# Self edges of a three-layer relational GNN: from gathered rows to a mask on VectorE over the rows just made

## The chip, the cores and the metric

One core of one Trainium2 chip (trn2). The metric is the device time of one execution in microseconds, median of three runs. Engines: PE (TensorE), DVE (VectorE), ACT (ScalarE), POOL (GpSimd), SP (the sync engine, which issues DMAs).

## What is computed

N = 3125 nodes, D = 128 features, E = 103,125 edges sorted by destination, R = 16 relation types, H = 4 attention heads, three layers. The edge list is 50,000 random pairs in both directions and then one edge from each node to itself; the sort is stable, so in every node's list the self edge is the last one.

```python
for l in range(L):
    ht = jnp.einsum('nd,rdo->nro', h, W_rel[l])
    msg = ht[src, etype]
    h_rel = jax.ops.segment_sum(msg, dst, num_segments=n)
    h_rel = h_rel + h @ W_loop[l] + b_rel[l]
    z = (h @ W_gat[l]).reshape(n, H, DH)
    el = jnp.sum(z * attn_l[l], axis=-1)
    er = jnp.sum(z * attn_r[l], axis=-1)
    e = jax.nn.leaky_relu(el[src] + er[dst], 0.2)
    # softmax of e over the edges of each dst (with its maximum), alpha
    h_gat = jax.ops.segment_sum(alpha[:, :, None] * z[src], dst, num_segments=n)
    hc = jnp.concatenate([h_rel, h_gat + b_gat[l]], axis=1) @ W_fuse + b_fuse
    # layer 0 only: hc = hc * sigmoid([hc, mean edge weight] @ W_gate + b_gate)
    h = jax.nn.relu(hc)
```

The output is layernorm(x + h).

## The kernel before

A table in HBM holds, for each node and type, a row of 260 floats: the 128 of the message ht, then for each head 32 of z and its el. An edge is one gathered row. Two tables alternate: layer l reads `table[l % 2]`, and the next layer's is written while layer l runs.

Until about 214 us the kernel loads, counts degrees, ranks the nodes by degree (descending), writes the first table tile by tile (PE, ACT, SP), gathers each node's list of edges, masks the lists (L1262 to L1267) and scatters lists and node data to `meta_ranked` in order of rank (L561). From there on it runs three layers of 25 tiles of 128 ranked nodes (tile 0 has 64 nodes, each on two partitions, and its halves are merged). I count layers one, two and three (l = 0, 1, 2) and tiles from 0. A tile has as many slots as its largest degree (tile 0: half of it). For the drawn graph that is 29, 45, 42, 40, 39, 38, 37, 36, 36, 35, 35, 34, 33, 33, 32, 32, 31, 30, 30, 29, 28, 27, 26, 25, 23: 825 in all.

**POOL** (L683 to L715) issues one indirect DMA for each slot (`fetch`, L593 to L596): row k of the list of 128 nodes into slot k of a buffer. A tile is split into groups: H with 16 slots in the buffer `meta_nat`, where there are 32 slots or more M1 with 16 in `late`, and the rest (1 to 15) as T in `scratch`, the tail. The names in the profile are those of the buffers. Before a group it waits until VectorE has staged its list of indices (`stage_head`, `stage_mid`, `stage_tail`) and until the last group in that buffer is summed (`free`). Behind H, from tile 2 on, it issues the store of the next layer's rows of two tiles earlier (`store_tile`, L671), in layers one and two.

**VectorE** in each tile (L1475 to L1513): clears the tail's slots and stages the tail's list (`stage_this_tail`, L1337), copies er (`start_tile`), runs `group` for H, then `epilogue` of the tile before (in layer one the gate, in layer three the layernorm), then `group` for M1 and T. A group waits for its gathers, computes logits and their maximum, carries the sums so far in slot 0, sums the messages (L1371), multiplies z by the weights that ACT put in PSUM (L1377) and sums that (L1381). T is computed for 15 slots, or for 8 where it has 8 or fewer. `end_tile` (L1396 to L1401) hands the sums to PE, with the loop term of `meta` added.

**ACT** gives each group its exponentials (`group`, L786), and in each tile the chain of the tile before: transposed sums, fused, gate, and `next_rows` (L810), which empties PE's table of the next layer into `rows[0]` and lets POOL store it. Through a layer's end this chain is passed once with nothing beside it: the next layer gathers only when all rows are stored (L723).

The wait that sets the tail's place on POOL is this:

```python
pool.wait_ge(s_tail, n_tile)     # L701, stage_tail written by VectorE
...
with pool.If(bits(pool, n, PAIR - 1) > 0):
    free("T")
    gather_tail(l, n, PAIR // 2)
```

## Time and profile before

| | |
|---|---|
| median of 3 runs | 3485.82 us (3484.82 to 3485.93) |
| the profiled execution: span, first to last instruction | 3490.2 us |
| its own device time | not listed apart; the span stands for it |
| POOL busy | 2489.3 us, 71% |
| VectorE busy | 2380.3 us, 68% |
| PE, ACT busy | 689.4 us, 424.8 us |
| gathers (indirect DMAs of L594) | 2475: 1200 + 720 + 555 |
| layers one, two, three | 214 to 1316 us, 1316 to 2412 us, 2412 us to the end |

POOL's busy time counts the making of each DMA's descriptors only, and the idle time between two DMAs issued back to back is told as "issue". The profiled execution is 4.4 us, 0.13%, above the median.

### The profile page before, as it was taken

How to read it: one execution, taken by the hardware profiler on the slowest of the kernel's cores; microseconds unless marked ns; L12 is line 12 of the kernel's file. 1: busy time of each engine (PE TensorE's matmuls, PEld its weight loads, DVE VectorE, ACT ScalarE, POOL GpSimd, SP SyncE). 2: the span in 40 equal slices, each digit the busy share in tenths (PEclk: the TensorE clock that was granted, in tenths of full speed). 3: DMA queues.
4: the chain of work that ended last, by engine and by line, in shares of the span. 5: the costliest groups of instructions: out<-in, count | busy, mean ns of one | idle time of the engine just before them, and what ended most of it. 6: DMA issues, size and time to landing. Idle time of an engine off the chain costs nothing.

```text
span 3490.2 us, 18122 instructions
## 1 busy us (share of the span) xinstructions
PE 689.4 (20%) x1897; PEld 372.5 (11%) x1897; DVE 2380.3 (68%) x3226; ACT 424.8 (12%) x769; POOL 2489.3 (71%) x2642
## 2 busy tenths in 40 slices
PE   8942111222122230011121111221000000000000
PEld 5421000111011110000000000110000000000000
DVE  8536666677676764665777756674776788877786
ACT  3530110111111120101111111111000000000000
POOL 1457777777777756777777777775777777777776
PEclk9965555555655555555555555555555555555555
DMA  7774444455545544444454544454433333333332
GB/s 271 315 249 129 134 147 152 152 151 152 152 152 159 168 145 118 130 151 152 151 152 151 153 152 152 152 173 140 107 106 107 107 106 107 106 106 107 106 103 74
DMA packets 143244, 505.96 MB, mean 145 GB/s; under 512 B 44277, under 2 KB 51002, under 8 KB 133618
## 3 DMA queue, kind: packets, MB, share of 16 engines
q0 software_dynamic: 130032, 444.45, 43.4%
q1 hardware_dynamic: 13186, 61.24, 4.5%
q14 instruction: 19, 0.16, 0.0%
q8 instruction: 7, 0.11, 0.0%
HBM read 341.05 MB, written 164.51 MB: 145 GB/s over the span
## 4 chain that ended last, share of the span: by engine, by line
POOL 45%; issue 29%; DVE 10%; DMA 6%; PE 4%; POOLq 3%; DVEq 1%; ACT 1%; SPq 1%; ACTq 0%
POOL meta_nat L594 20%; POOL late L594 14%; POOL scratch L594 10%; DVE acc L1381 3%; PE ps_table L886 1%; DMA late<-table,stage_mid 1%; DMA table<-rows 1%; DMA scratch<-table,stage_tail 1%; DVE late L1377 1%; DVE scratch L1377 1%; DVE meta_nat L1377 1%; POOLq L369 1%; POOL table L671 1%; DMA meta_nat<-table,stage_head 1%; PE ps_cnt L919 1%
## 5 line engine op out<-in xcount | busy, mean ns | idle before, releaser
L594 POOL DMA_INDIRECT meta_nat<-table,stage_head x1200 | 1139.0, 949 | 395.7 <-issue 385.3
L594 POOL DMA_INDIRECT late<-table,stage_mid x720 | 681.9, 947 | 219.4 <-issue 217.9
L594 POOL DMA_INDIRECT scratch<-table,stage_tail x555 | 525.9, 948 | 175.5 <-issue 175.2
L1025 PE MATMUL ps_mix<-ident,hr 128*128 128x128 f32 x75 | 35.5, 473 | 1991.2 <-DVE hg L1401 1991.2
L788 ACT ACTIVATE ps_cnt<-logit 128x68 f32<-128x68 f32 x189 | 43.7, 231 | 2767.1 <-DVE logit L1363 2766.1
L1381 DVE TENSOR_REDUCE acc<-meta_nat 128x132 f32<-128x2112 f32 x75 | 290.6, 3875 | 8.1 <-DVE meta_nat L1377 0.5
L1371 DVE TENSOR_REDUCE acc<-meta_nat 128x128 f32<-128x2048 f32 x75 | 282.6, 3767 | 0.0
L1049 PE MATMUL ps_table<-wrel,hT 128*128 128x512 f32 x400 | 266.4, 828 | 0.0
L1353 DVE TENSOR_TENSOR raw<-late,er_cur 128x64 f32<-128x64 f32 x45 | 12.0, 267 | 324.5 <-DMA late<-table,stage_mid 324.5
L1025 PEld LDWEIGHTS ps_mix<-ident,hr 128*128 128x128 f32 x75 | 13.6, 182 | 2039.8 <-DVE hg L1401 2039.8
L1381 DVE TENSOR_REDUCE acc<-scratch 128x132 f32<-128x1188 f32 (+1 forms) x69 | 208.7, 3024 | 7.1
L1353 DVE TENSOR_TENSOR raw<-meta_nat,er_cur 128x64 f32<-128x64 f32 x75 | 20.1, 267 | 281.6 <-DMA meta_nat<-table,stage_head 280.2
L1371 DVE TENSOR_REDUCE acc<-scratch 128x128 f32<-128x1152 f32 (+1 forms) x69 | 204.9, 2970 | 8.8
L1381 DVE TENSOR_REDUCE acc<-late 128x132 f32<-128x2244 f32 x45 | 183.3, 4072 | 4.7
L1371 DVE TENSOR_REDUCE acc<-late 128x128 f32<-128x2176 f32 x45 | 178.2, 3961 | 5.5
L1334 DVE MEMSET scratch<- 128x1024 f32 (+1 forms) x75 | 93.0, 1240 | 125.5 <-issue 125.5
L1377 DVE TENSOR_TENSOR meta_nat<-meta_nat,ps_cnt 128x2112 f32<-128x2112 f32 x75 | 175.8, 2344 | 3.1 <-ACT ps_cnt L788 3.1
L742 ACT ACTIVATE rows<-ps_table 128x1024 f32<-128x1024 f32 x150 | 148.8, 1026 | 100.2 <-PE ps_table L886 62.4
L1049 PEld LDWEIGHTS ps_table<-wrel,hT 128*128 128x128 f32 x400 | 115.3, 288 | 136.6 <-issue 126.3
L1377 DVE TENSOR_TENSOR scratch<-scratch,ps_cnt 128x1188 f32<-128x1188 f32 (+1 forms) x69 | 127.2, 1843 | 0.0
L1377 DVE TENSOR_TENSOR late<-late,ps_cnt 128x2244 f32<-128x2244 f32 x45 | 111.7, 2482 | 0.0
L1031 PE MATMUL ps_mix<-hrT,wfuse 128*128 128x128 f32 x100 | 39.8, 501 | 363.6 <-ACT hgT L794 363.6
(237 smaller groups left out, 1701.4 us busy)
## 6 DMA issues: line engine op xcount, KB each, us to landing
table<-rows SPq DMA_DIRECT2D x25, 2080.0 KB, 7.7
meta_nat<-table,stage_head POOLq DMA_INDIRECT x1200, 2.8
late<-table,stage_mid POOLq DMA_INDIRECT x720
scratch<-table,stage_tail POOLq DMA_INDIRECT x555, 2.8
meta<-meta_ranked SPq DMA_DIRECT2D x1, 2438.0 KB, 15.1
wrel<-in_L_gnn_W_rel POOLq DMA_DIRECT2D x2, 1024.0 KB, 13.5
meta_nat<-in_x SPq DMA_DIRECT2D x1, 832.0 KB, 18.4
table<-rows,stage_id POOLq DMA_INDIRECT x50, 7.8
```

Source lines behind the costliest of these rows:

```text
L369: n = eng.value_load(tile_slots[0:1, bass.ds(t, 1)], min_val=PAIR, max_val=E)
L594: pool.indirect_dma_start(out=slots[b][:, k, :], out_offset=None, in_=table[l % 2], in_offset=bass.IndirectOffsetOnAxis(ap=index, axis=0)) ...
L671: pool.indirect_dma_start(out=table[(l + 1) % 2][0:NP_ * R, :].rearrange("(n r) f -> n (r f)", r=R), out_offset=bass.IndirectOffsetOnAxis( ...
L742: return s.activation(rows[k][:, j * R // 2:(j + 1) * R // 2, 0:D], ps_table[:, 1024 * j:1024 * j + 1024].rearrange("p (r f) -> p r f", f= ...
L788: s.activation(wgt[:, :, :, 0], logit[:], ACT.Exp).then_inc(s_wgt, 1)
L1025: pe.transpose(mix[0], hr[:], ident[:])
L1031: pe.matmul(mix[2], wfuse[:, 0], hrT[:], start=True, stop=False)
L1049: mm = pe.matmul(ps_table[:, 512 * c:512 * c + 512], hT[0][:], wrel[:, l + 1, c * RC * D:(c + 1) * RC * D], start=True, stop=True)
L1334: v.memset(messages("T", 1, slots_of_tail + 1), 0.0)
L1371: v.tensor_reduce(acc[:, 0:D], messages(b, lo, K + 1).rearrange("p k d -> p d k"), AX.X, ALU.add).then_inc(s_part, 1)
L1377: v.tensor_tensor(weighted(b, lo, K + 1), weighted(b, lo, K + 1), wgt[:, lo:K + 1].to_broadcast([P, K + 1 - lo, H, EX]), ALU.mult).then_in ...
L1381: v.tensor_reduce(acc[:, D:ROW], slots[b][:, lo:K + 1, D:ROW].rearrange("p k f -> p f k"), AX.X, ALU.add).then_inc(s_acc, 1)
```

## The change

Four things, word for word below. First, before the layers VectorE finds in each list of rank 128 and above the last entry, tests that it is the node's own, takes it out of the list and out of the degree, and puts it in a new column `M_OWN`. Second, layer one gathers that column as a group of one into slot 0 of H (`gather_head`), so H has 17 slots there. Third, layers two and three do not gather it: ACT keeps z of each tile's nodes in `own_z` (which takes the place of `rows[1]`), VectorE copies it into slot 0 at the tile's start, and at the end of each tile but the first, ahead of `end_tile`, `add_own_messages` multiplies the finished `rows[0]` of the tile before by a one-hot of each node's own type, sums over the 16 types and adds the result to the loop term of the next layer. Fourth, ACT runs `next_rows` ahead of the third group's exponential instead of behind it, and waits there until VectorE's mask has read the rows. For tile 0's nodes (ranks below 128) nothing is taken out. `yo` moves into the room of `wrel`.

```diff
+            def gather_head(l):
+
+                if l == 0:
+                    pool.indirect_dma_start(
+                        out=slots["H"][:, 0, :], out_offset=None, in_=table[l % 2],
+                        in_offset=bass.IndirectOffsetOnAxis(ap=stage_head[:, 0:1], axis=0)).then_inc(s_own_landed, 16)
+                gather(l, "H", stage_head[:, 1:PAIR + 1])
...
                 free("H")
-                gather(l, "H", stage_head)
+                gather_head(l)
                 if l < L - 1:
                     with pool.If(t > 1):
                         store_tile(l)
...
                     act.reg_add(n_stored, n_stored, 16)
+                    act.wait_ge(s_own_rows, n_own)
+                    act.reg_add(n_own, n_own, 1)
                     act.wait_ge(s_z_ps, n_tab)
                     s.activation(rows[0][:, :, D:ROW], bc(ps_z[:, 0:D + H], R), ACT.Copy)
                     for j in range(2):
                         evacuate_half(0, j)
+                    s.activation(own_z[:, bass.ds(t, 1), :], ps_z[:, 0:D + H].rearrange("p (o f) -> p o f", o=1), ACT.Copy)
                     s.activation(meta[:, bass.ds(t, 1), M_ER:META],
                                  ps_z[:, D + H:ZW].rearrange("p (o f) -> p o f", o=1), ACT.Copy).then_inc(s_rows, 1)
                     act.reg_add(n_tab, n_tab, 1)
 
...
                 with act.If(groups > 1):
                     group()
-                    with act.If(groups > 2):
-                        group()
                 if not first:
                     next_rows(l, act.snap(n_last, min_val=0, max_val=T - 1))
                     act.reg_add(n_last, n_last, 1)
+                with act.If(groups > 2):
+                    group()
...
+            step(v.tensor_scalar(may_drop, rank[:], float(P), None, ALU.is_ge))
             for i, (t0, t1) in enumerate(ELL_CHUNKS):
+                lists, codes = meta_nat[:, t0:t1, M_ELL:SCATTERED], last_codes[:, 0:t1 - t0]
+                code, gap, own, gone = (a[:, t0:t1] for a in (last_code, apart, is_own, dropped))
                 dve.wait_ge(s_ell[i], 16 * (t1 - t0))
-                step(v.scalar_tensor_tensor(meta_nat[:, t0:t1, M_ELL:SCATTERED], ell_int[:, t0:t1], -float(NULL),
-                                            ell_valid[:, t0:t1], ALU.add, ALU.mult))
-                v.tensor_scalar(meta_nat[:, t0:t1, M_ELL:SCATTERED], meta_nat[:, t0:t1, M_ELL:SCATTERED], float(NULL), None,
...
-                                ALU.add).then_inc(s_ell_ok, 1)
...
+                step(v.scalar_tensor_tensor(lists, ell_int[:, t0:t1], -float(NULL), ell_valid[:, t0:t1], ALU.add, ALU.mult))
+                step(v.tensor_tensor(codes, lists, is_last[:, t0:t1], ALU.mult))
+                step(v.tensor_reduce(code, codes, AX.X, ALU.add))
+                step(v.tensor_tensor(gap, code, own_at[:, t0:t1], ALU.subtract))
+                step(v.tensor_tensor(gone, gap, gap, ALU.mult))
+                step(v.scalar_tensor_tensor(own, gone, 0.25 * R * R, may_drop[:, t0:t1], ALU.is_lt, ALU.mult))
+                step(v.tensor_tensor(gone, code, own, ALU.mult))
+                v.tensor_tensor(codes, is_last[:, t0:t1], bc_last(gone, ELL), ALU.mult)
+                step(v.tensor_tensor(degree[:, t0:t1], degree[:, t0:t1], own, ALU.subtract))
+                v.tensor_scalar(meta_nat[:, t0:t1, M_OWN], gone, float(NULL), None, ALU.add)
+                v.tensor_copy(meta_nat[:, t0:t1, M_CNT], degree[:, t0:t1])
+                v.scalar_tensor_tensor(lists, lists, float(NULL), codes, ALU.add, ALU.subtract).then_inc(s_ell_ok, 1)
...
-            def group(b, first=False, meanwhile=None, K=PAIR):
-
-                lo = 1 if first else 0
+            def group(b, first=False, meanwhile=None, K=PAIR, own_gathered=False):
+
+                lo = 1 if first and not own_gathered else 0
+                new = 0 if first else 1
                 dve.wait_ge(s_landed[b], n_land[b])
                 if b != "T":
                     dve.reg_add(n_land[b], n_land[b], 16 * K)
+                if own_gathered:
+                    dve.wait_ge(s_own_landed, n_own_land)
+                    dve.reg_add(n_own_land, n_own_land, 16)
...
                 dve.wait_ge(s_product, n_g)
-                v.tensor_reduce(acc[:, D:ROW], slots[b][:, lo:K + 1, D:ROW].rearrange("p k f -> p f k"), AX.X, ALU.add
...
             def start_tile(l, t):
                 if l == 0:
                     dve.wait_ge(s_er, n_t)
+                else:
+                    z = own_z[:, bass.ds(t, 1), :].rearrange("p o (h e) -> p (o h) e", e=EX)
+                    v.tensor_copy(weighted("H", 0, 1)[:, 0, :, 0:DH], z[:, :, 0:DH])
+                    v.tensor_scalar(weighted("H", 0, 1)[:, 0, :, DH], z[:, :, DH], no_own[:, bass.ds(t, 1)], None, ALU.add)
                 v.tensor_copy(er_cur[:], meta[:, bass.ds(t, 1), M_ER:M_LOOP]).then_inc(s_tile, 1)
                 dve.wait_ge(s_tile, n_t)
...
+            def add_own_messages(l, t):
+
+                if l < L - 1:
+                    dve.wait_ge(s_rows, n_rows)
+                    dve.reg_add(n_rows, n_rows, 1)
+                    v.tensor_tensor(own_rows[:], rows[0][:, :, 0:D],
+                                    own_hot[:, bass.ds(t, 1), :].rearrange("p o (r f) -> p (o r) f", f=1
+                                                                           ).to_broadcast([P, R, D]), ALU.mult
+                                    ).then_inc(s_own_rows, 1)
+                    dve.wait_ge(s_own, n_own)
+                    dve.wait_ge(s_own_rows, n_masked)
+                    dve.reg_add(n_masked, n_masked, 1)
+                    v.tensor_reduce(own_sum[:], own_rows[:].rearrange("p r d -> p d r"), AX.X, ALU.add
+                                    ).then_inc(s_own_sum, 1)
+                    dve.wait_ge(s_own_sum, n_own)
+                    dve.reg_add(n_own, n_own, 1)
+                    loop = meta[:, bass.ds(t, 1), M_LOOP:META].rearrange("p o f -> p (o f)")
+                    v.tensor_tensor(loop, loop, own_sum[:], ALU.add).then_inc(s_own, 1)
...
-                group("H", first=True, meanwhile=lambda: stage_next_head(t))
+                group("H", first=True, meanwhile=lambda: stage_next_head(t), own_gathered=l == 0)
                 if not first:
                     epilogue(l, dve.snap(n_last, min_val=0, max_val=T - 1))
-                    dve.reg_add(n_last, n_last, 1)
...
                     merge_halves(l)
+                else:
+                    add_own_messages(l, dve.snap(n_last, min_val=0, max_val=T - 1))
+                    dve.reg_add(n_last, n_last, 1)
                 end_tile(t)
...
                 epilogue(l, T - 1)
+                add_own_messages(l, T - 1)
```

Names with `own_` that are not shown are buffers and semaphores. With the last entry taken out of each list, tiles 1 to 24 have one slot less each (44, 41, 39, 38, 37, 36, 35, 35, 34, 34, 33, 32, 32, 31, 31, 30, 29, 29, 28, 27, 26, 25, 24, 22), 801 with tile 0.

VectorE, the end of a tile in the loop over tiles of layer one; before:

```order
L1377 TENSOR_TENSOR scratch<-scratch,ps_cnt 128x9x132 [waits weights_ready,peak_kept]
L1381 TENSOR_REDUCE acc<-scratch 128x132 [waits weighted_z_ready,messages_summed]
L1383 REGISTER_ALU
L1509 UNCONDITIONAL_BRANCH
L1396 RECIPROCAL rden<-acc 128x4 [waits sums_updated]
L1397 ISA
L1397 TENSOR_TENSOR hr<-acc,meta 128x128
L1400 REGISTER_ALU [waits denominators_inverted]
L1401 TENSOR_TENSOR hg<-acc,rden 128x128
```

and now:

```order
L1435 TENSOR_TENSOR scratch<-scratch,ps_cnt 128x9x132 [waits weights_ready,peak_kept]
L1439 TENSOR_REDUCE acc<-scratch 128x132 [waits weighted_z_ready,messages_summed]
L1441 REGISTER_ALU
L1594 UNCONDITIONAL_BRANCH
L1475 ISA [waits rows_ready]
L1476 TENSOR_TENSOR own_rows<-rows,own_hot 128x2048
L1482 REGISTER_ALU [waits own_messages_masked,own_messages_added_to_loop_term]
L1483 TENSOR_REDUCE own_sum<-own_rows 128x128
L1486 ISA [waits own_messages_summed]
L1488 TENSOR_TENSOR meta<-meta,own_sum 128x128
L1600 REGISTER_ALU
L1458 RECIPROCAL rden<-acc 128x4 [waits sums_updated]
```

Three instructions on 2048, 2048 and 128 elements and a wait for ACT's rows stand between the last group and `end_tile`; the rows of tail staging for the next tile come behind them all.

ACT, from the second group's exponential to the end of `next_rows` in the same loop; before:

```order
L788 ACTIVATE ps_cnt<-logit 128x68 [waits logits_ready]
L789 REGISTER_ALU
L838 COMPARE_AND_BRANCH
L788 ACTIVATE ps_cnt<-logit 128x68 [waits logits_ready]
L789 REGISTER_ALU
L838 UNCONDITIONAL_BRANCH
L814 REGISTER_ALU [waits rows_stored]
L816 ACTIVATE rows<-ps_z 128x16x132 [waits z_product_ready]
L742 ACTIVATE rows<-ps_table 128x8x128 [waits table_chunk1_ready]
L742 ACTIVATE rows<-ps_table 128x8x128 [waits table_chunk3_ready]
L819 ISA
L819 ACTIVATE meta<-ps_z 128x132
```

and now:

```order
L816 ACTIVATE ps_cnt<-logit 128x68 [waits logits_ready]
L817 REGISTER_ALU
L868 UNCONDITIONAL_BRANCH
L842 REGISTER_ALU [waits rows_stored]
L844 REGISTER_ALU [waits own_messages_masked]
L846 ACTIVATE rows<-ps_z 128x16x132 [waits z_product_ready]
L770 ACTIVATE rows<-ps_table 128x8x128 [waits table_chunk1_ready]
L770 ACTIVATE rows<-ps_table 128x8x128 [waits table_chunk3_ready]
L849 ISA
L849 ACTIVATE rows<-ps_z 128x132
L850 ISA
L850 ACTIVATE meta<-ps_z 128x132
```

The exponential of the third group (the second L788 row of before) has moved behind `next_rows`, which has a wait and a copy more.

## Rows read from the trace of the kernel before

**Rows 1.** The page: busy time by engine, and POOL's tenths in 40 slices.

```profile
PE 689.4 (20%) x1897; PEld 372.5 (11%) x1897; DVE 2380.3 (68%) x3226; ACT 424.8 (12%) x769; POOL 2489.3 (71%) x2642
...
POOL 1457777777777756777777777775777777777776
```

**Rows 2.** The page's costliest groups: the gathers by buffer (busy, mean ns | idle).

```profile
L594 POOL DMA_INDIRECT meta_nat<-table,stage_head x1200 | 1139.0, 949 | 395.7 <-issue 385.3
L594 POOL DMA_INDIRECT late<-table,stage_mid x720 | 681.9, 947 | 219.4 <-issue 217.9
L594 POOL DMA_INDIRECT scratch<-table,stage_tail x555 | 525.9, 948 | 175.5 <-issue 175.2
```

**Rows 3.** POOL's timeline, layer two, tiles 17 and 18 (start, length).

```profile
2133.70 0.94 POOL L594 DMA_INDIRECT scratch<-table,stage_tail  x1 [0.30 <-issue]
...
2153.70 0.95 POOL L594 DMA_INDIRECT meta_nat<-table,stage_head  x1 [0.30 <-issue]
2154.95 0.99 POOL L671 DMA_INDIRECT table<-rows,stage_id  x1 [0.30 <-issue]
2156.25 0.97 POOL L594 DMA_INDIRECT scratch<-table,stage_tail  x1 [0.30 <-issue]
```

**Rows 4.** VectorE's timeline in the same stretch.

```profile
2136.46 0.26 DVE L1353 TENSOR_TENSOR raw<-scratch,er_cur 128x60 f32<-128x60 f32 x1 [7.26 <-DMA scratch<-table,stage_tail]
...
2148.11 0.18 DVE L1396 RECIPROCAL rden<-acc 128x4 f32<-128x4 f32 x1
...
2152.13 0.13 DVE L1344 CAST stage_tail<-meta 128x15 uint32 x1
```

**Rows 5.** POOL's timeline, layer three, tile 22.

```profile
3372.20 0.94 POOL L594 DMA_INDIRECT meta_nat<-table,stage_head  x1 [0.30 <-issue]
3374.81 0.94 POOL L594 DMA_INDIRECT scratch<-table,stage_tail  x1 [1.67 <-issue]
```

**Rows 6.** VectorE's timeline, layer three, tiles 21 and 22.

```profile
3340.47 0.27 DVE L1353 TENSOR_TENSOR raw<-meta_nat,er_cur 128x64 f32<-128x64 f32 x1 [2.25 <-DMA meta_nat<-table,stage_head]
...
3357.59 0.26 DVE L1353 TENSOR_TENSOR raw<-scratch,er_cur 128x60 f32<-128x60 f32 x1 [0.30 <-issue]
...
3373.20 0.13 DVE L1344 CAST stage_tail<-meta 128x15 uint32 x1
```

**Rows 7.** Groups of VectorE's instructions, shapes apart.

```profile
L1371 DVE TENSOR_REDUCE acc<-meta_nat 128x128 f32<-128x2048 f32 x75 | 282.6, 3767 | 0.0
...
L1377 DVE TENSOR_TENSOR meta_nat<-meta_nat,ps_cnt 128x2112 f32<-128x2112 f32 x75 | 175.8, 2344 | 3.1 <-ACT ps_cnt L788 3.1
...
L1397 DVE TENSOR_TENSOR hr<-acc,meta 128x128 f32<-128x128 f32 x75 | 22.1, 295 | 0.2 <-issue 0.2
...
L1206 DVE TENSOR_REDUCE rank<-scratch 128x4 f32<-128x512 f32 x6 | 4.1, 680 | 0.0
```

**Rows 8.** VectorE's timeline before layer one: two-input comparisons and products.

```profile
113.69 2.23 DVE L1174 TENSOR_TENSOR late<-iota_slot,degree 128x2000 bf16<-128x2000 f32 x1
...
159.24 0.81 DVE L1270 TENSOR_TENSOR scratch<-scratch,degree 128x625 f32<-128x625 f32 x1
```

**Rows 9.** POOL's timeline in the same stretch.

```profile
114.85 1.92 POOL L549 DMA_INDIRECT meta_nat<-edge_rows,start_u  x1 [0.30 <-issue]
...
159.45 1.44 POOL L561 DMA_INDIRECT meta_ranked<-meta_nat,rank_u  x1 [0.30 <-issue]
```

**Rows 10.** POOL's timeline, the end of layer two.

```profile
2350.83 0.94 POOL L594 DMA_INDIRECT meta_nat<-table,stage_head  x1 [1.67 <-DVE acc L1381]
...
2390.09 0.99 POOL L671 DMA_INDIRECT table<-rows,stage_id  x1 [9.48 <-ACT meta L819]
2402.91 0.98 POOL L671 DMA_INDIRECT table<-rows,stage_id  x1 [11.83 <-ACT meta L819]
2411.80 0.98 POOL L594 DMA_INDIRECT meta_nat<-table,stage_head  x1 [7.90 <-issue]
```

**Rows 11.** POOL's timeline, the first gather of layer one.

```profile
214.45 0.95 POOL L594 DMA_INDIRECT meta_nat<-table,stage_head  x1 [11.28 <-issue]
```

More of the change, by code:

```diff
@@ L21 @@
 LEAST = -1.0e37
+SHUT = -1.0e34
 SLOPE = 0.2
@@ L1376, in group @@
                 dve.wait_ge(s_wgt, n_g)
[L1377 to L1378 removed]
+                v.tensor_tensor(weighted(b, 0, K + 1), weighted(b, 0, K + 1),
+                                wgt[:, 0:K + 1].to_broadcast([P, K + 1, H, EX]), ALU.mult).then_inc(s_product, 1)
                 dve.wait_ge(s_part, n_g)
                 dve.wait_ge(s_product, n_g)
[L1381 removed]
+                v.tensor_reduce(acc[:, D:ROW], slots[b][:, 0:K + 1, D:ROW].rearrange("p k f -> p f k"), AX.X, ALU.add
                                 ).then_inc(s_acc, 1)
```

73 lines of the change are left out of this document (53 added, 20 removed).

## The prediction

> **What bounds the kernel.** The page comes first: POOL is busy for 71% and VectorE for 68% of the span [rows 1], so busy shares do not name the bound. The groups do: POOL's 2475 gathers take 948 ns each, and the idle time ahead of them is nearly all "issue", some 0.32 us each, hardly ever a wait for data or for VectorE [rows 2]. In POOL's timeline the starts stand 1.25 us apart, from one buffer to the next and past a store (1.30 us) [rows 3]. So POOL never stops within a layer, and the three layers last as long as their gathers: (2475 + 46 stores) × 1.25 = 3150 us of the 3490. The rest is the work before the first gather [rows 11], the last tile's way to the output, and two layer ends, where the last rows must be stored before the next layer gathers: from the store of tile 23 to that of tile 24 and to the next gather, 2390.09 to 2411.80 us [rows 10].
>
> The second reading is how far VectorE is from POOL, and it belongs to a place. In a tile of 32 slots or more POOL comes to the tail after 16 gathers for H and 16 for M1. In a tile of fewer it comes there straight after H, and needs VectorE's list of the tail, which VectorE writes only after the tail, sums and end of the tile before. In layer two: last tail gather at 2133.70, VectorE begins that group at 2136.46, ends its sums at 2148.11, and has the next list at 2152.13 plus 0.13 us; POOL's next tail gather is at 2156.25 [rows 3, 4]. In layer three, where the epilogue is longer and no store is in between, the cover is already gone: the list is there at 3373.33, the gather comes at 3374.81, after 1.67 us idle instead of 0.30 [rows 5, 6]. So from list to gather it takes 1.48 us, and in layer two VectorE is early by 2156.25 − 1.48 − 2152.26 = 2.5 us. That small cover is what the change must fit into.
>
> **The parts, and their cost.**
>
> Gathers. Tiles 1 to 24 lose one slot: 24 less in each layer, and layer one gets 25 for the own rows. 47 less × 1.25 us = −59 us [rows 2, 3].
>
> What of that is not worth its price. Where VectorE sets the pace already, a gather less buys nothing. In layer three a late tile takes VectorE 3373.33 − 3340.47 = 32.9 us [rows 6], against (16 + tail) × 1.25: under 27 slots POOL is the faster. In layers one and two POOL waits for H's sums at the last tile (1.67 us in layer two [rows 10]). Some 13 gathers of late tiles lie there: +16. H has 17 rows of z instead of 16, 132 elements more in two instructions at 1.1 and 1.8 ns each [rows 7], and the tile starts with two small copies, 0.8 us a tile in all, on the path only in those tiles: +3.
>
> The addition at a tile's end. The mask works on 2048 elements; the product with 2112 takes 2344 ns [rows 7], so 2.27 us. The sum over types reads with a stride, 16 values for each of 128 results, as the sum of the messages does: 3.77 us. The addition on 128: 0.3 us. Each waits for the one ahead, about 0.1 us: together 6.6 us, in 24 tiles and once at the end of layers one and two. The reduction I could not see with this stride (512 bytes, the messages' is 1040). Bounds: at the rate of a reduction of contiguous values, 680 ns for 512 [rows 7], it takes 2.7 us and the whole 5.5; half as slow again gives 8.5. I take 3.77, as inner length and results are the same.
>
> Where it lies. With M1 in between, POOL has 20 us more to do and doesn't feel it. From tile 14 to 23 it does, because add_own_messages stands ahead of end_tile and the staging. Layer two: 6.6 − 2.5 = 4.1 us wait. In layer one H has a gather more, 1.25: 2.8 us. (Tile 24 comes behind a tail of 8, 4.3 us shorter for VectorE, and is spared.) 10 tiles × 6.9 = +69.
>
> Layer ends. The addition for tile 23 stands ahead of tile 24's end_tile, and ACT copies z once more (0.3 us) before the rows are ready: 2 × 6.9 = +14. While POOL waits for tail lists it no longer waits for H: −6. The addition for tile 24 runs beside the store and the first 16 gathers of the next layer, 8.9 + 20 us [rows 10]: nothing.
>
> The mask beside the gathers. The stretch before layer one shows something that the layers don't: a VectorE product or comparison with both inputs in SBUF stops an indirect DMA that POOL begins beside it [rows 8, 9]. The one at 114.85 begins 1.07 us before such an instruction ends (113.69 + 2.23 = 115.92) and takes 1.92 us, 0.97 over the usual; the one at 159.45 begins 0.60 before the end at 160.05 and takes 1.44, 0.49 over. So it is held to the end, less 0.1 us. The products in the layers (L1377) take their weights from PSUM, and the mean of 949 ns [rows 2] leaves no room for such holds. The mask has both inputs in SBUF, and at 2.27 us it is longer than the pitch, so one gather always begins inside, 1.02 to 2.27 us before its end: 1.5 us on average. In tiles 14 to 23 the wait for the list swallows it (the hold comes in H, ahead of that wait). In tiles 2 to 13 and 24, 13 a layer, POOL is the bound: 26 × 1.5 = +39. On this the Trainium skill speaks otherwise. SBUF — State Buffer, "Who interferes with whom", says that a two-input VectorE instruction contends only with GpSimd instructions that read SBUF, and infers from a probe, in which tensor_tensor did not stall a DMA, that making descriptors needs the write interface alone. By that the +39 would be 0. The two DMAs of [rows 8, 9] are against it; perhaps since these DMAs read a list of indices.
>
> ACT. next_rows ahead of the third exponential: the table is complete some 20 us after H begins, M1's group comes 20 us behind H, and the tail's logits 13 us later still; nothing waits. In tiles of two groups nothing moves.
>
> Before layer one. Each of three chunks of lists gets some nine small instructions, about 4.5 us, before its scatters. The tables bound this stretch, and POOL has 7 us to spare between the staged head and 214.45 [rows 11]; the first chunk and a few held scatters use it up: +2, between 0 and 6.
>
> **Sum**: −59 + 16 + 3 + 69 + 14 − 6 + 39 + 2 = +78 us. That is against the profiled execution of 3490.2, 0.13% over the median; on the median, 3485.8 + 78 = **3564 us**, 2.2% slower.
>
> **Rivals.**
>
> *No hold.* Everything as above, but the mask doesn't stop POOL. For it: no row of a layer shows a hold, and only two DMAs before them do, of other kinds (lists, a scatter). Against: both lengths fit the rule to 0.03 us. Then 3564 − 39 = **3525**. By the Trainium skill's inference this is what would come.
>
> *VectorE's additions are covered: faster.* VectorE is idle for 32%, and gets 50 × 6.6 = 330 us, 9% of the span. If its idle time were free to be used, only the layer ends would remain: −59 + 16 + 3 + 14 + 2 = −24, **3462**. It decides where the addition is under 2.5 us, the cover in [rows 3, 4]. For it: the busy shares, and POOL's tenths show nobody waited for [rows 1]. Against: mask alone is 2.3 us by any row. With the addition at 5.5 us and no hold the waits are 3.0 and 1.7: 3490, about no change.
>
> *Dearer.* The strided sum at 1.5 times my price, or a mask stopped in turn by POOL: the addition is 8.5 us, waits 6.0 and 4.8 in ten tiles, layer ends 4 more: +42, **3606**. The rows show no VectorE instruction lengthened by POOL.
>
> *The entries are not dropped.* Were a node's last entry not recognised, the tiles would keep their slots, the head would gather 25 rows more, and the adding would run on zeros: 3564 + 60 − 16 = **3608**. Against: the self edge is last in each list, and the test allows exactly the node's 16 rows.
>
> **How the numbers follow.** Both mechanisms, 3564: 0.62, with a range of its own of 3540 to 3590 (hold between 1.0 and 2.0 us, the addition 6.0 to 7.2). No hold, 3525: 0.16. Covered, in whole or nearly: 0.08, half of it near no change. Dearer: 0.12. Not dropped: 0.02. A measurement here tells 0.2%, 7 us, from no change. Faster: 0.06; same: 0.03; slower: 0.91. The range for 8 in 10 takes in the first two cases and half of the dearer one: 3512 to 3602.
>
> **What would show it.** On the page of the changed kernel: 2428 gathers; the reduction of 128x2048 from own_rows near 3.8 us, 50 of them, and the mask near 2.3. In POOL's timeline, tiles 14 to 23 of layers one and two: ahead of the first tail gather 2 to 3 us idle in layer two and about 1 to 2 in layer one, told as "issue", 1.48 us after stage_tail; no such wait from tile 2 to 13. In the same tiles one gather of H near 2.5 us instead of 0.95, beginning inside the mask: one in each tile from 2 on, none in layer three. Layer three itself about 25 us shorter. The stores at the layer ends some 20 us apart instead of 13. I am wrong in the large if no head gather is long (then 3525), if POOL shows no idle ahead of the tails (then near 3500 or under), or if the waits also appear in tiles with M1.

## The result, and the profile after

| | before | changed |
|---|---|---|
| device time, median | 3485.32 us (3483.24 to 3485.93, 4 runs) | 3567.22 us (3566.19 to 3571.1, 4 runs) |
| the profiled execution's span | 3490.2 us | 3564.6 us |
| first to last gather, layers one, two, three | 1064.6, 1064.0, 1038.8 us | 1115.2, 1092.6, 1013.8 us |
| last gather to the next layer's first | 36.6, 32.1 us | 46.8, 41.7 us |

The changed kernel takes 1.0236 times as long (95% interval 1.0224 to 1.0249): 82 us slower, where 78 were forecast. Of the two spans, the changed one is 74.4 us longer.

The page of the changed kernel, busy time by engine (for the kernel before: [rows 1]):

```profile
PE 692.4 (19%) x1897; PEld 371.7 (10%) x1897; DVE 2681.9 (75%) x3453; ACT 432.0 (12%) x813; POOL 2515.3 (71%) x2595
```

VectorE has 302 us more, and POOL 26 us more although it issues 47 gathers fewer. The groups of POOL's instructions tell why (busy, mean ns | idle; for the kernel before: [rows 2]):

```profile
L614 POOL DMA_INDIRECT meta_nat<-table,stage_head x1200 | 1201.0, 1001 | 389.3 <-issue 374.1
L614 POOL DMA_INDIRECT late<-table,stage_mid x624 | 591.4, 948 | 190.1 <-issue 187.7
L614 POOL DMA_INDIRECT scratch<-table,stage_tail x579 | 548.1, 947 | 223.7 <-issue 221.2
...
L625 POOL DMA_INDIRECT meta_nat<-table,stage_head x25 | 23.7, 947 | 19.4 <-DVE stage_head L1344 8.0 <-issue 6.7 <-DVE acc L1439 4.7
```

The head's gathers went from a mean of 949 ns to 1001 ns, and the others did not. The idle time ahead of the tail's went from 175.5 to 223.7 us for 24 gathers more, which at 0.30 us each explain 7. So both prices are on the page: DMAs held in H, and waits ahead of T. VectorE's new groups:

```profile
L1483 DVE TENSOR_REDUCE own_sum<-own_rows 128x128 f32<-128x2048 f32 x50 | 178.9, 3578 | 9.4 <-DVE own_rows L1476 9.3
...
L1476 DVE TENSOR_TENSOR own_rows<-rows,own_hot 128x2048 f32<-128x2048 f32 x50 | 114.1, 2283 | 17.7 <-ACT meta L850 17.6
```

Where the time goes can be seen in one tile. POOL's timeline of the changed kernel, layer two, tile 18 (start, length, [idle before]):

```profile
2223.20 0.95 POOL L614 DMA_INDIRECT meta_nat<-table,stage_head  x1 [0.30 <-issue]
2224.46 2.40 POOL L614 DMA_INDIRECT meta_nat<-table,stage_head  x1 [0.30 <-issue]
2227.16 0.95 POOL L614 DMA_INDIRECT meta_nat<-table,stage_head  x1 [0.30 <-issue]
...
2232.16 0.99 POOL L699 DMA_INDIRECT table<-rows,stage_id  x1 [0.30 <-issue]
2235.81 0.96 POOL L614 DMA_INDIRECT scratch<-table,stage_tail  x1 [2.66 <-issue]
```

and VectorE's in the same stretch, the end of tile 17 and the start of tile 18:

```profile
2219.97 3.86 DVE L1439 TENSOR_REDUCE acc<-scratch 128x132 f32<-128x2112 f32 x1
2223.75 2.28 DVE L1476 TENSOR_TENSOR own_rows<-rows,own_hot 128x2048 f32<-128x2048 f32 x1
2226.22 3.58 DVE L1483 TENSOR_REDUCE own_sum<-own_rows 128x128 f32<-128x2048 f32 x1 [0.19 <-DVE own_rows L1476]
2229.98 0.29 DVE L1488 TENSOR_TENSOR meta<-meta,own_sum 128x128 f32 x1 [0.18 <-DVE own_sum L1483]
...
2232.57 1.66 DVE L1388 MEMSET scratch<- 128x1920 f32 x1 [1.79 <-issue]
2234.21 0.13 DVE L1398 CAST stage_tail<-meta 128x15 uint32 x1
```

Two things are to be seen. The gather begun at 2224.46 falls inside the mask (2223.75 to 2226.03) and takes 2.40 us instead of 0.95: it is held 1.45 us, and the mask had 1.57 us to go. And the addition (2223.75 to 2230.27, 6.5 us) puts the list at 2234.34; POOL's first tail gather comes 1.47 us behind it, after 2.66 us of idle time instead of 0.30. In the kernel before, the same two events were 1.48 us apart where POOL had to wait [rows 5, 6]; in this tile POOL was the later one there [rows 3, 4].

Over the whole trace, 49 of the 50 masks have a DMA of POOL beginning inside, and each of these 49 is long: 44 gathers by 65.4 us together, and 5 stores by 5.9. Each ends its hold 0.11 to 0.14 us before the mask does. By place, from POOL's timelines of all tiles (us; a wait is the idle time over 0.30 ahead of the group's first gather):

| | holds of gathers | waits for the tail's list |
|---|---|---|
| layer one, tiles 14 to 23 | 17.2 | 12.8 |
| layer two, tiles 14 to 23 | 15.3 | 26.4 |
| layers one and two, other tiles | 32.9 | 0.0 |
| layer three | 0.0 | 6.3 (before: 6.1) |

The five held stores are not in this table: two stand in tiles 10 and 11 of layer two, in the place of a held gather, and three at the layer ends.

At the layer ends the stores of tiles 23 and 24 stand further apart. POOL's timeline, end of layer two (for the kernel before: [rows 10]):

```profile
2483.71 0.99 POOL L699 DMA_INDIRECT table<-rows,stage_id  x1 [11.19 <-ACT meta L850]
2503.90 1.44 POOL L699 DMA_INDIRECT table<-rows,stage_id  x1 [19.19 <-issue]
2513.29 0.98 POOL L614 DMA_INDIRECT meta_nat<-table,stage_head  x1 [7.96 <-issue]
```

20.2 us instead of 12.8 from store to store, and the last store is itself held 0.45 us by the mask that runs as soon as the same rows are ready; in layer one it is 21.1 instead of 14.3, and the hold 1.46.

### The profile page after: what moved, and what is told of

Same layout as the page of the kernel before. It is cut to its first block, busy times and chain, and to the rows that moved or that the text cites. A ratio compares the mean times of both kernels' runs of the same rounds, so it can differ in the third digit from the quotient of the medians.

```text
span 3564.6 us, 18765 instructions
## 1 busy us (share of the span) xinstructions
PE 692.4 (19%) x1897; PEld 371.7 (10%) x1897; DVE 2681.9 (75%) x3453; ACT 432.0 (12%) x813; POOL 2515.3 (71%) x2595
## 4 chain that ended last, share of the span: by engine, by line
POOL 40%; issue 31%; DVE 12%; DMA 8%; PE 4%; POOLq 2%; DVEq 1%; ACT 1%; SPq 1%; ACTq 0%
POOL meta_nat L614 19%; POOL late L614 12%; POOL scratch L614 7%; DVE acc L1439 2%; DMA late<-table,stage_mid 2%; DMA meta_nat<-table,stage_head 2%; DVE late L1435 2%; PE ps_table L918 1%; DVE meta_nat L1435 1%; DMA table<-rows 1%; DMA scratch<-table,stage_tail 1%; DVE own_sum L1483 1%; DVE scratch L1435 1%; PE ps_cnt L951 1%; POOLq L389 1%
## 5 line engine op out<-in xcount | busy, mean ns | idle before, releaser
L614 POOL DMA_INDIRECT meta_nat<-table,stage_head x1200 | 1201.0, 1001 | 389.3 <-issue 374.1
L614 POOL DMA_INDIRECT late<-table,stage_mid x624 | 591.4, 948 | 190.1 <-issue 187.7
L614 POOL DMA_INDIRECT scratch<-table,stage_tail x579 | 548.1, 947 | 223.7 <-issue 221.2
L1439 DVE TENSOR_REDUCE acc<-meta_nat 128x132 f32<-128x2244 f32 x75 | 306.6, 4089 | 7.7
L1429 DVE TENSOR_REDUCE acc<-meta_nat 128x128 f32<-128x2048 f32 (+1 forms) x75 | 288.2, 3843 | 0.0
L1439 DVE TENSOR_REDUCE acc<-scratch 128x132 f32<-128x2112 f32 (+1 forms) x69 | 213.5, 3094 | 7.1
L1429 DVE TENSOR_REDUCE acc<-scratch 128x128 f32<-128x2048 f32 (+1 forms) x69 | 208.7, 3024 | 8.8
L1388 DVE MEMSET scratch<- 128x1920 f32 (+1 forms) x75 | 95.3, 1270 | 135.1 <-issue 135.1
L1435 DVE TENSOR_TENSOR meta_nat<-meta_nat,ps_cnt 128x2244 f32<-128x2244 f32 x75 | 186.2, 2482 | 0.0
L1483 DVE TENSOR_REDUCE own_sum<-own_rows 128x128 f32<-128x2048 f32 x50 | 178.9, 3578 | 9.4 <-DVE own_rows L1476 9.3
L1435 DVE TENSOR_TENSOR scratch<-scratch,ps_cnt 128x2112 f32<-128x2112 f32 (+1 forms) x69 | 130.1, 1885 | 0.0
```

Source lines behind the costliest of these rows:

```text
L614: pool.indirect_dma_start(out=slots[b][:, k, :], out_offset=None, in_=table[l % 2], in_offset=bass.IndirectOffsetOnAxis(ap=index, axis=0)) ...
L1388: v.memset(messages("T", 1, slots_of_tail + 1), 0.0)
L1429: v.tensor_reduce(acc[:, 0:D], messages(b, lo, K + 1).rearrange("p k d -> p d k"), AX.X, ALU.add).then_inc(s_part, 1)
L1435: v.tensor_tensor(weighted(b, 0, K + 1), weighted(b, 0, K + 1), wgt[:, 0:K + 1].to_broadcast([P, K + 1, H, EX]), ALU.mult).then_inc(s_prod ...
L1439: v.tensor_reduce(acc[:, D:ROW], slots[b][:, 0:K + 1, D:ROW].rearrange("p k f -> p f k"), AX.X, ALU.add).then_inc(s_acc, 1)
L1483: v.tensor_reduce(own_sum[:], own_rows[:].rearrange("p r d -> p d r"), AX.X, ALU.add).then_inc(s_own_sum, 1)
```

## The experiments

Twelve runs. They fell on two kinds of surroundings, which has to be said first. On three chips the kernel before took 3965 to 3973 us, on two others, an hour later, 3486 and 3490 us, as in the result. Each ratio below is to the kernel before as measured on the same chip. No chip was measured at both times, so the runs don't tell the chip from the hour; "these chips" below means these chips at that time.

### On the chips where before takes about 3970 us

The first batch, all edits of the changed kernel. The mask in PSUM, so that the product has one input there:

```diff
-        own_hot = sb("own_hot", [P, T, R])
...
+        own_hot = ps_cnt[:, 512 - T * R:512].rearrange("p (t r) -> p t r", r=R)
```

> The changed kernel with own_hot in free columns of the PSUM bank ps_cnt, so the mask has one input in SBUF. If a product with two SBUF inputs holds the gather that begins beside it: no gather of H is longer than 1.1 us any more, the waits for the tail's list grow by what the holds had swallowed (to about 4 us in layer two), and the kernel takes about 3525 us (3515 to 3535). Rival, the mask holds POOL for another reason (its length, its writes, ACT's copies at that time): the long gathers stay and the time is 3567 within 5.

The addition behind the tile's end:

```diff
-                else:
+                end_tile(t)
+                if not first:
                     add_own_messages(l, dve.snap(n_last, min_val=0, max_val=T - 1))
                     dve.reg_add(n_last, n_last, 1)
-                end_tile(t)
```

> The changed kernel with add_own_messages behind end_tile instead of ahead of it; the tail's list is still staged behind it. My theory: the waits of POOL in tiles 14 to 23 stay as they are, and only the two layer ends get shorter, by about 6.6 us each: about 3554 us (3548 to 3560). Rival, the layer ends did not grow by the addition (it ran in the time in which PE and ACT worked anyway): 3567 within 4. Rival, the waits come from the late sums (hr, hg) and not from the late list: the idle time ahead of the tail gathers goes, 3500 to 3525.

The addition of tile t − 2 at the start of tile t, behind the staging of the tail's list and start_tile (`late_add` is true in layers one and two; the last two additions stand at the layer's end):

```diff
                 start_tile(l, t)
+                if late_add:
+                    add_own_messages(l, own_tile)
+                    dve.reg_add(n_own_tile, n_own_tile, 1)
...
-                else:
-                    add_own_messages(l, dve.snap(n_last, min_val=0, max_val=T - 1))
...
-                with dve.Fori(1, T) as t:
-                    tile(l, t)
+                tile(l, 1)
+                with dve.Fori(2, T) as t:
+                    tile(l, t, late_add=l < L - 1)
+                add_own_messages(l, T - 2)
```

> The changed kernel with the addition of a tile two back at the start of each tile, behind the staging of the tail's list and ahead of the H group. My theory: POOL's waits for the list (41 us in all, 3.6 and 2.3 us a tile) go, the layer ends shorten by about 13, but the holds by the mask that these waits swallowed now count: about 3518 us (3505 to 3530). Rival, VectorE is simply too busy in the late tiles and the place doesn't matter: 3550 to 3567.

No addition at all (the own messages are missing from the output, all else runs):

```diff
-                    v.tensor_tensor(own_rows[:], rows[0][:, :, 0:D],
...
-                    v.tensor_tensor(loop, loop, own_sum[:], ALU.add).then_inc(s_own, 1)
+                    dve.sem_inc(s_own_rows, 1)
```

> The changed kernel without mask, sum and addition on VectorE (the own messages of layers two and three are left out of the result; everything else stays). My theory: no holds, no waits in layers one and two, layer ends as before: about 3448 us (3435 to 3460), which is the worth of the 47 gathers less what late tiles and the 17th row take back. Rival, most of the loss sits in the other parts (17 rows in H, copies at the tile's start, ACT's order, lists): 3480 or more.

Then on a second chip the changed kernel itself as a yardstick, the mask in PSUM again, and two edits of the kernel *before*: an idle product of 2048 elements in every tile, its second input in SBUF in one and in PSUM in the other:

```diff
+            def spare():
+                dve.wait_ge(s_spare, n_spare)
+                dve.reg_add(n_spare, n_spare, 1)
+                v.tensor_tensor(room1[:, 16:32], room1[:, 0:16], null_row[:, 0:D].rearrange("p (o f) -> p o f", o=1
+                                ).to_broadcast([P, 16, D]), ALU.mult).then_inc(s_spare, 1)
```

(with `ps_cnt[:, 136:136 + D]` in place of `null_row[:, 0:D]` in the other).

> The changed kernel as it is, as a yardstick on the chip of these runs. Where the kernel before takes about 3485 us, both theories expect 3560 to 3575 us, ratio 1.022 to 1.026, with holds of about 36 us in layer one and 28 us in layer two. If the chip is again one on which the kernel before takes about 3970 us: there VectorE lost time at every branch (idle before the first instruction of each tile 353 us against 135), so list waits reach all tiles and the addition's 6.6 us would cost more than on the first chip, ratio 1.00 to 1.03.

> The changed kernel with the mask in PSUM, so that the product of the addition has one SBUF and one PSUM input. Theory (a gather begun beside a product of two SBUF inputs waits until it ends; VectorE's 6.6 us make the tail lists late): holds go to zero, gathers without waits 946 to 949 ns mean, list waits grow to 3 to 4 us in tiles 14 to 23 of layers one and two; the time falls from the changed kernel's by 30 to 50 us, to about 3525 us where the kernel before takes 3485. Rival A (the long gathers are something else, the memory's reads or stores): holds stay, time as the changed kernel's within 5 us. Rival B (holds only take time that would be waited for the list anyway, all of it): holds vanish, time falls by less than 10 us.

> The kernel before, and in each of its 75 tiles one idle product of 2048 elements on VectorE with two inputs in SBUF, after the tile's first part, that nobody needs (about 2.3 us each). Theory of the hold: in nearly every tile one gather beside it takes 2 to 3 us instead of 0.95; 60 to 75 times 1.0 to 1.5 us, so 60 to 110 us above the same kernel with one input of the product in PSUM, and 60 to 150 us above the kernel before. Rival (no hold by operands, only VectorE's lateness counts): the two spare kernels take the same within 5 us.

> The kernel before, and in each of its 75 tiles one idle product of 2048 elements on VectorE with one input in SBUF and one in PSUM, in the same place as in the other spare kernel. Theory: no gather beside it is longer than 0.96 us on account of it, and the time is that of the kernel before plus what VectorE's 2.3 us do where its tail list is on the path: 0 to 50 us, and 60 to 110 us below the kernel whose spare product has two SBUF inputs. Rival (no hold by operands): as the other spare kernel within 5 us.

And on a third, mask in PSUM and list first together:

> The changed kernel with the mask in PSUM and the addition of tile t - 2 moved behind the staging of tile t, so that the tail list is there before VectorE begins it. Theory (the price of the addition is the hold of the gathers plus the lateness of the tail list): on a chip where the kernel before takes about 3485 us and the changed one about 3567, no gather longer than 0.96 us, nearly no wait for the tail list in tiles 14 to 22, and 3440 to 3475 us, faster than both kernels: what is left is 59 us of gathers saved, given back in part by later heads and the two extra ends of layers. Rival (the addition costs by its length on VectorE wherever it stands): 3510 to 3530 us, as with the mask in PSUM alone. On a chip where the kernel before takes about 3970 us VectorE bounds most tiles, and both expect a ratio of 0.995 to 1.005.

Measured:

| run | median, us | ratio to before, 95% interval |
|---|---|---|
| mask in PSUM | 3963.22 | 0.9978 (0.9955 to 1.0001) |
| addition behind the tile's end | 3944.92 | 0.9923 (0.9896 to 0.995) |
| list first | 3988.91 | 1.0044 (1.0026 to 1.0061) |
| no addition | 3916.93 | 0.9854 (0.9828 to 0.9881) |
| changed kernel as it is | 3959.47 | 0.9982 (0.9957 to 1.0008) |
| mask in PSUM, again | 3955.28 | 0.9966 (0.9942 to 0.9991) |
| spare product, two SBUF inputs | 3969.93 | 1.0011 (0.9988 to 1.0034) |
| spare product, one in PSUM | 3969.56 | 1.0002 (0.998 to 1.0025) |
| mask in PSUM and list first | 4003.16 | 1.0078 (1.0055 to 1.0102) |

In times, both theories missed here: the changed kernel is as fast as the kernel before. The forecasts made for such chips were missed too, if by little: 1.00 to 1.03 for the changed kernel (0.9982 came), 0.995 to 1.005 for mask in PSUM and list first (1.0078). The changed kernel's trace shows where the time goes. Busy lengths are those of the result's trace, but VectorE stands still where nothing releases it. VectorE's group at the start of a tile, in the result's trace:

```profile
L1388 DVE MEMSET scratch<- 128x1920 f32 (+1 forms) x75 | 95.3, 1270 | 135.1 <-issue 135.1
```

and the same kernel's on the slower chip:

```profile
L1388 DVE MEMSET scratch<- 128x1920 f32 (+1 forms) x75 | 95.3, 1270 | 321.4 <-issue 321.4
```

One such place, VectorE's timeline of the same run, layer one:

```profile
703.61 0.29 DVE L1463 TENSOR_TENSOR hg<-acc,rden 128x128 f32<-128x128 f32 x1 [0.66 <-issue]
716.56 0.91 DVE L1388 MEMSET scratch<- 128x1024 f32 x1 [12.67 <-issue]
...
719.71 0.17 DVE L1452 COPY er_cur<-meta 128x4 f32 x1 [1.92 <-issue]
723.91 0.27 DVE L1411 TENSOR_TENSOR raw<-meta_nat,er_cur 128x68 f32<-128x68 f32 x1 [4.03 <-issue]
```

Behind the loop's branch VectorE stands for up to 13 us, where in the result's trace it is 1.45 to 2.54. With the addition removed the same group stands for 480.1 us instead of 321.4: of the 325 us (50 times 6.5) that it is spared, it stands 159 longer in this place. So VectorE with its gaps sets the pace in many tiles there, and POOL waits: in the changed kernel's layer one 92 us ahead of heads and 40 ahead of tails, against 4 and 13 in the result's trace. That is why these chips can show whether a DMA is held, but not what that costs on the others.

Whether it is held they show sharply. In the yardstick 48 of 50 masks hold a DMA, gathers by 65.1 us together; with the mask in PSUM 88 gathers and stores begin inside masks, and none is held. The edits of the kernel before show it for an instruction that is not the addition. VectorE's and POOL's timelines with two SBUF inputs:

```profile
2126.90 2.29 DVE L1396 TENSOR_TENSOR rows<-rows,null_row 128x2048 f32<-128x2048 f32 x1 [2.57 <-issue]
```

```profile
2126.62 0.94 POOL L595 DMA_INDIRECT late<-table,stage_mid  x1 [0.30 <-issue]
2127.87 2.14 POOL L595 DMA_INDIRECT late<-table,stage_mid  x1 [0.30 <-issue]
2130.31 0.94 POOL L595 DMA_INDIRECT late<-table,stage_mid  x1 [0.30 <-issue]
```

and with one in PSUM:

```profile
2092.59 2.29 DVE L1396 TENSOR_TENSOR rows<-rows,ps_cnt 128x2048 f32<-128x2048 f32 x1 [2.62 <-issue]
```

```profile
2092.46 0.95 POOL L595 DMA_INDIRECT late<-table,stage_mid  x1 [0.30 <-issue]
2093.71 0.95 POOL L595 DMA_INDIRECT late<-table,stage_mid  x1 [0.30 <-issue]
2094.97 0.94 POOL L595 DMA_INDIRECT late<-table,stage_mid  x1 [0.30 <-issue]
```

The products are equally long. In the first trace the gather begun at 2127.87 is held 1.2 us of the product's last 1.32; the one begun at 2126.62, before the product, is not held. In the second two gathers begin inside and neither is. In the first 3600 us, 61 gathers are held by 84 us in the one, against 7 that are 0.2 us longer on average in the other. (In that second trace 65 DMAs that begin outside the products are longer than their kind too, so these 7 need not be holds.) And the times are the same to 0.4 us: the 84 us of POOL's time cost nothing where POOL was not the bound. What it is not held, it waits: ahead of the groups' first gathers POOL waits 425 us with one input in PSUM and 343 with two in SBUF. The expected 60 to 110 us between the two were wrong for that reason.

### On the chips where before takes about 3490 us

The mask in PSUM and the addition behind the tile's end, together (on a chip where before took 3486.42 us):

> The changed kernel with the mask in PSUM and the addition behind the tile's end instead of ahead of it. Where the kernel before takes 3485 us: theory (holds and late tail lists are two prices) 3510 to 3525 us: the holds gone, the list waits of tiles 14 to 23 as long as with the mask in PSUM alone (3 to 4 us), layer ends each 3 to 7 us shorter. Rival (only where the addition stands counts): 3540 to 3560. Where the kernel before takes 3970 us and VectorE bounds most tiles: the end of the tile alone gave 0.992 and the mask in PSUM 0.997 of the kernel before, the changed kernel itself 0.998; if the two gains add, 0.990 to 0.992; if the hold costs nothing there, as the two spare kernels say, no change against the end of the tile alone: 0.991 to 0.994.

Measured 3518.46 us (3517.77 to 3521.0), ratio 1.0092 (1.0075 to 1.0109). Then on another chip (before 3489.99 us) the two that separate the prices; the edits are those shown above.

> The changed kernel with the mask in PSUM, again, since the kernel before takes about 3485 us now. Theory: holds gone; 39 us of them were on the path (tiles 2 to 13 and 24 and the last stores), the rest was swallowed by list waits, which grow by as much (tiles 14 to 23: 45 to 50 us in layer two instead of 26, 28 to 34 in layer one instead of 13): 3520 to 3535 us, ratio 1.010 to 1.014. Rival A (all holds, 71 us, were on the path): 3490 to 3505. Rival B (holds cost nothing): 3560 to 3570. Against the run with the addition behind the tile's end as well (3518): 3 to 15 us slower.

> The changed kernel with the mask in PSUM and the addition of tile t - 2 behind the staging of tile t, again, since the kernel before takes about 3485 us now. Theory (the price of the addition is holds plus late tail lists): no gather longer than 1.1 us, nearly no wait for the tail list in tiles 14 to 22, 3440 to 3475 us, faster than both kernels. Rival (the addition costs by its length on VectorE wherever it stands, and later heads take back what earlier lists give): 3500 to 3530 us.

| run | median, us | ratio, 95% interval | holds | waits for tail lists, tiles 14 to 23, layers one, two | gaps between layers |
|---|---|---|---|---|---|
| changed kernel | 3567.22 | 1.0236 (1.0224 to 1.0249) | 71.3 | 12.8, 26.4 | 46.8, 41.7 |
| mask in PSUM | 3530.6 | 1.0114 (1.0098 to 1.0131) | 0 | 28.4, 40.9 | 44.5, 42.0 |
| and behind the tile's end | 3518.46 | 1.0092 (1.0075 to 1.0109) | 0 | 29.1, 42.8 | 39.3, 36.4 |
| mask in PSUM and list first | 3463.01 | 0.9923 (0.9907 to 0.994) | 0 | 0.0, 0.0 | 40.3, 35.9 |

*Mask in PSUM* gives 37 us back of the 82 (by the medians; by the two ratios, each to before on its own chip, it is 43). Its page shows the head's gathers at their old length:

```profile
L614 POOL DMA_INDIRECT meta_nat<-table,stage_head x1200 | 1138.4, 949 | 390.0 <-issue 374.9
L614 POOL DMA_INDIRECT scratch<-table,stage_tail x579 | 549.1, 948 | 253.6 <-issue 253.0
```

The idle time of the tail's gathers grew in turn, from 223.7 to 253.6 us. Tile 18 of layer two shows how. POOL's and VectorE's timelines with the mask in PSUM:

```profile
2190.59 0.95 POOL L614 DMA_INDIRECT meta_nat<-table,stage_head  x1 [0.30 <-issue]
2191.84 0.95 POOL L614 DMA_INDIRECT meta_nat<-table,stage_head  x1 [0.30 <-issue]
...
2196.84 1.00 POOL L699 DMA_INDIRECT table<-rows,stage_id  x1 [0.30 <-issue]
2201.88 0.96 POOL L614 DMA_INDIRECT scratch<-table,stage_tail  x1 [4.05 <-issue]
```

```profile
2189.84 2.28 DVE L1476 TENSOR_TENSOR own_rows<-rows,ps_cnt 128x2048 f32<-128x2048 f32 x1
...
2200.28 0.14 DVE L1398 CAST stage_tail<-meta 128x15 uint32 x1
```

No gather is long beside the mask, and the wait for the list is 4.05 us instead of 2.66: what the hold took in the head, the wait had covered. Holds of 71.3 us went, waits of 30.1 came, 41 are left, and 37 to 43 us were measured. Rivals A and B (3490 to 3505, 3560 to 3570) are out. The forecast of 1.010 to 1.014 held, and so did that of layer one's list waits (28 to 34 us); layer two's came to 40.9 us, short of the 45 to 50 expected.

*Behind the tile's end* (with the mask in PSUM) leaves the list where it was, and the waits with it. It shortens each gap between layers by 5 to 6 us, because tile 24's sums reach PE before the addition. By the medians' ratios that is 0.2%, with intervals that overlap; the gaps in the traces show it, 10.8 us together.

*List first* (with the mask in PSUM) tests the other price: it moves no work off VectorE, which is busy 2688.6 us against 2683.2 with the mask in PSUM alone. POOL's and VectorE's timelines, tile 18 of layer two:

```profile
2143.92 0.99 POOL L699 DMA_INDIRECT table<-rows,stage_id  x1 [0.30 <-issue]
2145.22 0.96 POOL L614 DMA_INDIRECT scratch<-table,stage_tail  x1 [0.30 <-issue]
```

```profile
2133.18 3.86 DVE L1439 TENSOR_REDUCE acc<-scratch 128x132 f32<-128x2112 f32 x1
...
2141.17 0.14 DVE L1398 CAST stage_tail<-meta 128x15 uint32 x1
...
2141.78 2.29 DVE L1476 TENSOR_TENSOR own_rows<-rows,ps_cnt 128x2048 f32<-128x2048 f32 x1 [0.17 <-DVE er_cur L1452]
2144.27 3.58 DVE L1483 TENSOR_REDUCE own_sum<-own_rows 128x128 f32<-128x2048 f32 x1 [0.20 <-DVE own_rows L1476]
2148.02 0.29 DVE L1488 TENSOR_TENSOR meta<-meta,own_sum 128x128 f32 x1 [0.17 <-DVE own_sum L1483]
...
2163.67 0.26 DVE L1411 TENSOR_TENSOR raw<-scratch,er_cur 128x60 f32<-128x60 f32 x1 [3.60 <-DMA scratch<-table,stage_tail]
```

The list is written 4.3 us after the last sum of the tail instead of 10.5, and POOL, which comes at 2145.22, no longer waits. The addition is as long as before and stands beside gathers of the tail, for whose landing VectorE still waits 3.60 us. The time is 0.9923 of the kernel before: 27 us faster than it, and 68 us faster than with the mask in PSUM alone. The list waits of 69.3 us are nearly all of it, but not exactly: the gaps between layers are 10 us shorter as well, and POOL waits 13 us more ahead of heads in layers one and two. The rival of 3500 to 3530 us, a price by length wherever it stands, is out. Where every tile waits for VectorE it does not help: on the chip of about 3970 us the same kernel was slower than before, 1.0078, with POOL waiting 147 us ahead of layer one's heads.

Not tried alone: ACT's order, the column of own rows in layer one, and the work before the layers. The kernel without any addition was not run on the chips of 3490 us, so its forecast of 3448 us stands open.

## Why the prediction was right

The time is 3567 us against 3564, inside the likeliest case's own range, and both mechanisms were there. The steps, as measured, add up to 76 us against the spans' difference of 74.4. The sum is nearer than its terms: late tiles were 5 us too dear and the mask beside gathers 6, the tail lists 3 too cheap and the layer ends 6, and these nearly cancel. By the steps:

- **Gathers, −59.** The count is as forecast, 2428. Layer three has no addition and shows them best: 24 fewer, −30 us by the pitch, −25.0 measured, as forecast.
- **Late tiles, +16, 17th row and copies, +3, H waits, −6: +13 together.** Mis-sized: 5 in layer three, and 2.8 more waits ahead of heads in layers one and two, so 8 (no run tells these three terms apart). The waits for H's sums did not vanish, they grew. They stand in tile 13, just ahead of the stretch that waits for lists, and in tiles 23 and 24, at and behind its end.
- **Tail lists, tiles 14 to 23, +69.** Measured 71.7: holds of 32.5 and waits of 39.2. The trade inside, that the wait swallows the hold, was seen by itself in the run with the mask in PSUM, where the waits alone are 69.3. The addition took 6.5 us (forecast 6.6): mask 2283 ns for 2.27, sum 3578 for 3.77, priced from the messages' sum [rows 7].
- **The mask beside gathers, +39.** Mis-sized: 32.9 in the other tiles. 24 of the 26 had a held gather, at 1.37 us instead of 1.5; in the other two, tiles 10 and 11 of layer two, a store was held instead, by 0.95 and 0.96 us. "Held to the end, less 0.1 us", read off two DMAs [rows 8, 9], is 0.11 to 0.14 in 49 cases of 49. The inference of the Trainium skill (SBUF — State Buffer, "Who interferes with whom"), by which this term was 0, doesn't hold in this kernel: against it stand these 49 cases, the yardstick and the spare products. Whether it is the list of indices that these DMAs read, as I supposed, no run tells: none had a DMA without a list beside the mask. Nor were two DMAs all that could be seen before: in the trace of the kernel before 328 gathers and stores begin inside the layers' products with weights in PSUM, at least 0.15 us before their end, and none is longer for it, while the short copy of the sums (L1368, SBUF to SBUF, 0.29 us) makes 33 gathers 0.06 to 0.12 us longer. So "no row of a layer shows a hold" was not so.
- **Layer ends, +14.** Measured 19.8. The stores of tiles 23 and 24 are 6.8 and 7.4 us further apart (layers one and two); forecast were 6.9 each. The rest I had not counted: the hold takes the last store as well, since the mask starts when the same rows come ready (1.46 and 0.45 us), and tile 23's store stands 1.8 and 1.7 us further behind the layer's last gather.
- **Before layer one, +2.** 2.5: the first gather stands at 216.95 instead of 214.45 [rows 11]; VectorE begins the head's list at 215.90 instead of 207.46, so the spare time was used up, as said. In three runs with the same work ahead of it, it stood at 214.8 to 217.4, so this term is not told from a variation.
- **ACT's order, nothing.** The groups' products (L1435) show no idle time for ACT's weights in the changed kernel's trace. That fits; it was not tested by itself.

The rival No hold (3525) is what the mask in PSUM makes, 3530.6. Covered (3462) was ruled out by place, not by amount: with the same work on VectorE behind the list, the kernel is at 3463. That the two numbers agree is partly luck: in that kernel the gaps between layers grew by 7.5 us, not 14, and waits ahead of heads by 16. Dearer and Not dropped are out by the lengths and the count. Two of the rivals' sums were wrong by my own terms: with the addition at 5.5 us and no hold they give 3501, not 3490, and with no entry dropped 72 gathers come back, not 48, which gives 3638, not 3608. Neither case came.

What the prediction lacked is a condition: all of it holds where POOL sets the pace. On the chips where VectorE was slowed by gaps at its branches, the same edit moved nothing (0.9982).

## What to carry to other kernels

Price work on an engine that is not the bound by what it stands ahead of, not by its length: the same 300 us of VectorE work left this kernel 82 us slower where it stood ahead of a list of indices and held GpSimd's DMAs, and 27 us faster behind the list with its mask in PSUM. A large VectorE product with both inputs in SBUF holds nearly every indirect DMA that GpSimd begins beside it; put one input in PSUM where there is room, and look in the trace for DMAs longer than their kind. But count the saved time only where that DMA queue is the bound.

## What the runs showed of the hardware that was not expected

- The hold falls on whatever indirect DMA begins while the product runs, gathers and stores alike. A DMA already under way when the product begins is spared (36 in the changed kernel's trace), and so were five of those that began up to 0.04 us behind its start in the run with the addition behind the tile's end alone, and four up to 0.02 us behind it in the run with the spare product.
- It is not only products: the copy of the sums from SBUF to SBUF (0.29 us, one input) holds too: 33 of 40 gathers begun inside it took 1.01 to 1.07 us in the trace of the kernel before instead of 0.95, as if held to 0.12 or 0.13 us before its end. VectorE's reductions do not: in the trace of the kernel before 975 gathers and stores begin inside those of L1371 and L1381, at least 0.15 us before their end, and none is longer.
- An input in PSUM removes the hold and costs VectorE nothing: 2277 ns instead of 2283 for the mask, 2288 instead of 2295 for the spare product.
- The sum over types, 128 results of 16 values at a stride of 512 bytes, takes 3578 ns, 5% less than the messages' sum of the same shape with 1040 bytes [rows 7].
- The same program took 14% longer on three chips than on two others, with busy lengths alike and more idle time for which the trace shows no releaser: 672 us on VectorE instead of 143, 1855 on ACT instead of 4, by the timelines of the changed kernel. On VectorE the longest such gaps stand behind the loop's branch. The order of the variants turned over with it: list first was the slowest there and the fastest here. What makes these gaps is open; which chip a comparison ran on, and when, has to be told with it.
